# Two-layer recurrent block on one core: early loads by SyncE, v loaded by rows, the scatter in four parts, and the causal mask of the row maxima moved from TensorE to VectorE

## What is computed

```
xn = layernorm(x)                                     # 4096 tokens x 256
q, k, v = xn @ Wq.T, xn @ Wk.T, xn @ Wv.T             # 16 heads of 16
scores = q k^T / 4, masked so that key <= query       # 2 x 16 x 2048 x 2048
out = softmax(scores) @ v, then @ Wo.T
...
logits = xn @ router_w                                # 8 experts, the best one is taken
pos = running count of the tokens of that expert; kept if pos < 512
expert_in[expert, pos] += xn * kept                   # the scatter
hidden = gelu(expert_in @ w1); y = hidden @ w2        # gathered again by (expert, pos)
```

## Time and profile before

| | us |
|---|---|
| median of three executions | 2667.69 (2661.28 to 2670.05) |
| the profiled execution | 2670.18 |
| its span (first to last instruction) | 2668.5 |
| busy in the span: TensorE matmul, VectorE, ScalarE, GpSimd | 2428.0, 1847.2, 1410.9, 938.3 |
| mean granted TensorE clock | 0.952 of full speed |

### The profile page before, as it was taken

How to read it: one execution, slowest core, us unless ns; L and a number is a source line. 1 busy time by engine, 2 the same in 40 slices (tenths; PEclk the granted TensorE clock), 3 DMA queues, 4 the chain that set the end, 5 groups by cost and what they waited for, 6 DMA issues and landing times. The chain is left out here.

```text
span 2668.5 us, 46850 instructions
## 1 busy us (share of the span) xinstructions
PE 2428.0 (91%) x15908; PEld 1558.7 (58%) x15908; DVE 1847.2 (69%) x3682; ACT 1410.9 (53%) x2776; POOL 938.3 (35%) x936
## 2 busy tenths in 40 slices
PE   5778966999999999879967599999999999999999
PEld 4622322333333333268856477777777777777777
DVE  7688865888888888234347567767776777777676
ACT  3525534666666666756533355555555555555554
POOL 2330032110101101024334445555544555544553
PEclk9869978999999999989977799999999999999999
DMA  3850220403404030043266000000000000000000
GB/s 123 228 145 11 43 56 31 62 26 42 60 6 62 17 49 7 15 158 130 75 216 205 11 14 15 9 11 13 13 13 13 13 9 11 13 13 13 13 9 9
DMA packets 180617, 132.47 MB, mean 50 GB/s; under 512 B 91666, under 2 KB 167960, under 8 KB 180497
## 3 DMA queue, kind: packets, MB, share of 16 engines
q1 hardware_dynamic: 149872, 97.96, 14.9%
q0 software_dynamic: 6944, 20.37, 2.6%
q10 hardware_dynamic: 23680, 12.59, 1.8%
HBM read 84.43 MB, written 46.14 MB: 49 GB/s over the span
## 5 line engine op out<-in xcount | busy, mean ns | idle before, releaser
L915 DVE TENSOR_REDUCE a_best<-a_ring 128x1 f32<-128x512 f32 (+3 forms) x1280 | 699.3, 604 | 181.3 <-PE a_ring L716 95.9
L827 ACT ACTIVATE a_probs<-a_pss 128x1024 f32<-128x1024 f32 (+3 forms) x640 | 556.1, 896 | 419.6 <-PE a_pss L766 410.0
L1638 POOL TENSOR_TENSOR w_probs<-w_probs,w_inv 128x512 f32<-128x512 f32 x256 | 301.4, 1177 | 394.3 <-DVE w_inv L1897 385.0
L1803 ACT ACTIVATE w_probs<-w_pss,w_top 128x256 f32<-128x256 f32 x512 | 239.5, 477 | 378.2 <-DVE w_top L1891 363.8
L659 POOL TENSOR_SCALAR_AFFINE_SELECT a_probs<-a_probs 128x256 f32<-128x256 f32 x256 | 102.9, 408 | 785.6 <-ACT a_probs L827 783.8
L1661 PE MATMUL w_psw<-wqkv,w_xr 128*128 128x512 f32 x1152 | 300.5, 397 | 11.6 <-POOL w_xr L1595 11.6
L1701 PE MATMUL w_pss<-w_kd,w_qt 128*128 128x256 f32 x1536 | 277.7, 309 | 0.0
L1891 DVE TENSOR_REDUCE w_top<-w_pss 128x2 f32<-128x512 f32 x256 | 176.9, 691 | 140.6 <-PE w_pss L1701 139.6
L713 PE MATMUL a_ring<-g_kb,g_qa 96*128 96x512 bf16 (+3 forms) x640 | 229.6, 372 | 26.5 <-DVE a_best L915 13.0
L713 PE MATMUL a_ring<-a_kb,a_qa 96*128 96x512 bf16 (+3 forms) x640 | 218.4, 350 | 15.9 <-DVE a_best L915 12.0
L1661 PEld LDWEIGHTS w_psw<-wqkv,w_xr 128*128 128x128 f32 x1152 | 204.8, 189 | 47.4 <-POOL w_xr L1595 12.1
(11 more groups left out here) (233 smaller groups left out, 4187.6 us busy)
## 6 DMA issues: line engine op xcount, KB each, us to landing
e_w<-in_w SPq DMA_DIRECT2D x16, 1024.0 KB, 7.9
qk_parts<-p_parts SPq DMA_DIRECT2D x32, 384.0 KB, 3.9
a_qa<-qk_parts SPq DMA_DIRECT2D x96, 64.0 KB, 2.5
a_kb<-qk_parts SPq DMA_DIRECT2D x24, 256.0 KB, 9.3
g_qa<-qk_parts SPq DMA_DIRECT2D x72, 64.0 KB, 2.5
g_kb<-qk_parts SPq DMA_DIRECT2D x18, 256.0 KB, 8.7
p_xin<-in_x SPq DMA_DIRECT2D x8, 512.0 KB, 5.4
v_rows<-p_vout SPq DMA_DIRECT2D x8, 512.0 KB, 5.3
```

The costliest lines, as they stand in the source:

```text
L827: act.activation(probs[:, idx % 4, :, lo:CH], pss[idx % 2][:, :, lo:CH], ACT.Exp).then_inc(exp_done, 1)
L915: vec.tensor_reduce(best[:, i // TC, h * TC + i % TC, k:k + 1], bank[:, 0:keys], X, ALU.max).then_inc(ring_taken, 1)
L1638: pool.tensor_tensor(probs[:, p % 4, :, :], probs[:, p % 4, :, :], inv[:, :, p:p + 1].to_broadcast([P, 2, 2 * P]), ALU.mult).then_inc(p_re ...
L1803: ins = act.activation(probs[:, p % 4, e, :], pss[p % 2][:, e, :], ACT.Exp, bias=top[:, e, p:p + 1], accum_out=rows[:, e, p:p + 1])
```

## The change

It has four parts.

1. **Early loads.** (Both queues wait first for the stores of chunks 0 to 3.) The first group's loads are no longer issued by GpSimd behind chunk 5's copy, but by SyncE behind chunk 5's store, so ahead of the stores of chunks 6 and 7. TensorE waits once for all 30 of q and k, no longer chunk by chunk.
2. **v by rows, q by heads.** v is one DMA a group instead of four, with runs of 64 floats (256 bytes), into a new tile `v_rows`; GpSimd copies it to `vg` (`place_v`), once per group. q is still 24 DMAs of 64 KB, now one per head and part, not one per chunk and part. Order: k, q, v.
3. **Scatter in parts.** The 32 indirect DMAs go in four lots of 8, at the first step of the last query chunk of groups 3, 4, 5 and 6 (`SCATTER_AT`).
4. **Mask on VectorE.** The matmul L716 is gone. For a diagonal block VectorE reduces the keys ahead of the last 128 as before, if there are any, and then does `tensor_tensor_reduce` on the last 128: adds the float32 mask, writes the sum back to the bank, and takes the maximum into a fifth column of `best`.

```diff
-                if c == NC // B + 1:
...
-                    group_k(pool, dram, [early.kb], 0, early.k_landed)
-                    group_q(pool, dram, [early.qa], 0, early.q_landed)
-                    group_v(pool, dram, [early.vg], 0, early.v_landed)
...
                 store(c, c % 2)
+                if c == NC // B + 1:
...
+                    load_group(sp, dram, [early.qa], [early.kb], [early.v_rows], 0, early.qk_landed, early.v_landed)
...
+    for r, part in enumerate(PARTS_Q):
+        for h in range(GH):
+            eng.dma_start(qa[u][r * HD:(r + 1) * HD, :, h, :],
+                          dram["qk_parts"][0, part, first + h * HD:first + (h + 1) * HD, u * S:(u + 1) * S]
+                          .rearrange("d (c n) -> d c n", n=CH)).then_inc(qk_signal, 16)
+    eng.dma_start(rows[u][:, :, :], dram["v"][u * S:(u + 1) * S, first:first + GH * HD].rearrange("(j p) d -> p j d", p=P)
+                  ).then_inc(v_signal, 16)
...
+            def place_v(g):
+                u = g % 2
+                pool.wait_ge(v_loaded[u] if g else early.v_landed, 16 * ((g + 1) // 2) if g else 16)
+                pool.tensor_copy(vg[u][:, :, :, 0:HD], v_rows[u][:, :, :].rearrange("p j (h d) -> p j h d", d=HD)
+                                 ).then_inc(v_set, 1)
...
+                if s[0] == "S" and s[2:] == (QC - 1, 0, 0):
+                    g = s[1]
+                    if g + 1 < GROUPS:
+                        place_v(g + 1)
+                    if g in SCATTER_AT:
...
+                        for t in range(SCATTER_AT.index(g), NT, len(SCATTER_AT)):
+                            pool.indirect_dma_start(dram["expert_in"],
...
-                if diagonal:
-                    ins = pe.matmul(bank[:, keys - P:keys], keep["identity16"][:, :], keep["mask_qk"][:, :],
-                                    start=False, stop=True)
...
+                    if k < i // TC:
+                        vec.tensor_reduce(found[:, k:k + 1], bank[:, 0:keys], X, ALU.max).then_inc(ring_taken, 1)
+                    else:
+                        own = slice(keys - P, keys)
+                        if keys > P:
+                            vec.tensor_reduce(found[:, k:k + 1], bank[:, 0:keys - P], X, ALU.max)
+                        vec.tensor_tensor_reduce(out=bank[:, own], in0=bank[:, own], in1=keep["mask_qk"][:, :], scale=1.0,
+                                                 scalar=LOWEST, op0=ALU.add, op1=ALU.max, accum_out=found[:, QC:QC + 1]
+                                                 ).then_inc(ring_taken, 1)
```

More of the change, by code:

```diff
@@ L36 @@
 NEG = -1e30
+LOWEST = -3.0e38
 HD = D // H
@@ L317, in _ @@
                 store(c, c % 2)
+                if c == NC // B + 1:
+                    for u in range(2):
+                        for m in range(4):
+                            sp.wait_ge(parts_stored[u][m], 16 * NC // B // 2)
+                        sp.wait_ge(v_stored[u], 16 * NC // B // 2)
+                    load_group(sp, dram, [early.qa], [early.kb], [early.v_rows], 0, early.qk_landed, early.v_landed)
             for u in range(2):
@@ L464 @@
 ROUTE_COUNT, ROUTE_EXP = 6, 8
+SCATTER_AT = (3, 4, 5, 6)
 def attention_plan():
@@ L543, with load_group @@
 RING = 3
[L546 to L556, removed]
+def load_group(eng, dram, qa, kb, rows, g, qk_signal, v_signal):
     first, u = (g // 2) * GH * HD, g % 2
@@ L561, in group_k @@
                       dram["qk_parts"][1, part, first:first + GH * HD, u * S:(u + 1) * S]
[L562 to L571, removed]
+                      .rearrange("(h d) n -> d h n", d=HD)).then_inc(qk_signal, 16)
+    for r, part in enumerate(PARTS_Q):
[5 more added lines that the diff above has]
+                  ).then_inc(v_signal, 16)
 PARTS_Q, PARTS_K = (0, 0, 1, 1, 0, 2), (0, 1, 0, 1, 2, 0)
@@ L584, in __init__ @@
         self.vg = st.sb("vg0", [P, KT, GH, 32])
+        self.v_rows = st.sb("v_rows0", [P, KT, GH * HD])
         self.logits = st.sb("logits", [P, E, NT])
-        self.k_landed, self.v_landed = st.sem("k_landed"), st.sem("v_landed")
-        self.q_landed = [st.sem(f"q_landed{c}") for c in range(QC)]
+        self.qk_landed, self.v_landed = st.sem("qk_landed"), st.sem("v_landed")
         self.set_up = st.sem("set_up")
@@ L708, in a_step @@
                 keys = min(CH, (i + 1) * P - k * CH)
-                diagonal = k == i // TC
                 u, bank = g % 2, ring[r % RING]
                 wait(pe, ring_taken, r + 1 - RING)
-                ins = pe.matmul(bank[:, 0:keys], qa[u][0:QR, i // TC, h, (i % TC) * P:(i % TC + 1) * P],
-                                kb[u][0:QR, h, k * CH:k * CH + keys], start=True, stop=not diagonal)
-                if diagonal:
-                    ins = pe.matmul(bank[:, keys - P:keys], keep["identity16"][:, :], keep["mask_qk"][:, :],
-                                    start=False, stop=True)
-                ins.then_inc(ring_full, 1)
-            pe.wait_ge(early.k_landed, 16 * len(PARTS_K))
-            m = idx = pv = copied = chunk = 0
-            group, ones_seen = 0, -1
-            pe.wait_ge(early.q_landed[0], 16 * len(PARTS_Q))
+                pe.matmul(bank[:, 0:keys], qa[u][0:QR, i // TC, h, (i % TC) * P:(i % TC + 1) * P],
+                          kb[u][0:QR, h, k * CH:k * CH + keys], start=True, stop=True).then_inc(ring_full, 1)
+            pe.wait_ge(early.qk_landed, 16 * n_loads)
+            m = idx = pv = copied = group = 0
+            ones_seen = -1
             for s, r in plan:
@@ L726, in _ @@
                     _, g, h, i, k = s
-                    if g == 0 and i // TC != chunk:
-                        chunk = i // TC
-                        pe.wait_ge(early.q_landed[chunk], 16 * len(PARTS_Q))
                     if g != group:
```

51 lines of the change are left out of this document (19 added, 32 removed).

## The result

The changed kernel takes 2642.78 us (median of 5, 2641.44 to 2648.74), the kernel before beside it 2669.09 (5, 2661.28 to 2670.05): ratio 0.9911, 95% interval 0.9893 to 0.9929. The terms behind that number did not come out alike, though: one was right, two missed in opposite directions and nearly cancelled.

The account below looks back on a forecast made before the run. Neither VectorE nor TensorE was taken to rule an undisturbed group alone, each waiting for the other; the scatter left a 40.3 us hole. Scatter -40.3, loads -2 and mask +28 gave -14 us, hence 2653 us, range 2628 to 2700.

Parts of the forecast that it names:

- Scatter, -40.3 us: In the group with routing: GpSimd's scatter in lots fits its idle time, so PV's whole wait behind it goes, -40.3 us.
- Project and early loads, -2 us: End of project: chunks 4 and 5 run unhindered, but the last stores land behind the loads; -8 to +3, taken as -2 us.
- Rival 4: SyncE's queue: stores of chunks 6 and 7 land late behind the loads, project ends 8 us later; 2661 us, chance 0.06.
- Mask, +28 us: Attention's maxima: VectorE's added instructions cost 0.15 us a diagonal block, partly hidden, less TensorE's saved matmuls; +28 us together.
- r = 0.10: VectorE's accumulator read in each diagonal block, taken to cost 0.10 us, between bounds of 0.065 and 0.199.
- The other sign: Forecast is wrong if VectorE's pass of 128 columns takes more than 1.05 ns a column.
- e: Added VectorE time per diagonal block for the mask: 0.15 us forecast, bounds 0.11 and 0.25.
- TensorE's saving, half of 3.8 us a group: Undisturbed groups: dropping the mask matmuls frees 3.8 us of TensorE's queue a group, of which half was counted.
- Rival 1: VectorE's idle time swallows the mask in groups 1 to 6 at 0.11 us a diagonal block; 2624 us, chance 0.17.
- Rival 2: Accumulator read costs 0.15 us, a diagonal block 0.20 us, mask 44 us; gain and cost cancel at 2670 us, chance 0.14.
- rival 3: VectorE becomes the bound: read 0.20 us, diagonal block 0.25 us, mask +87 us; slower at 2712 us, chance 0.18.
- Rival 5: Scatter lots aren't covered because GpSimd reaches them late; 2653 us plus up to 20, chance 0.03.

## Why the prediction was right, and where it was not

- **Scatter, -40.3 us: right.** -41.8 at the experts' start with nothing else changed, -41.5 in the group itself. The hole goes whole, with the low clock behind it. In the changed kernel the lot of group 3 stands where it was said to: the v copy at 626.73 for 1.04 us, eight scatters from 627.93, 1.29 us apart.
- **Project and early loads, -2 us: wrong, it is +7.2.** The step that failed is the price of the stores behind the loads. I gave the stores behind the loads "2.74 and 1.1 us or up to 4.7 each" and had the last go out at 129 to 135; chunk 6's took 15.45 + 1.10 and the last went out at 143.94. The right price stood in my own: chunk 5's stores, issued beside the loads, take 13.94 us. I counted those 12 us as saved there and did not move them to the chunk that now comes behind the loads. The rest was as worked out: loads from 106.34 (107.4 said, with 4.7 for a chunk's stores where the rows give 2.74 + 1.10) to 122.28 (121 to 125 said). Rival 4 had the mechanism, with 8 us where 9 came. The barrier, "not above 145", was at about 149.3.
- **Mask, +28 us: right in sign, wrong in size; 9.6 to 11.5 by the traces, 11 to 15 by the medians.** The step that failed is the accumulator read: r = 0.10, about 0 found. The prediction's own sign, "wrong if the accumulator read isn't near 0.1 us", came true for the mechanism: its row says 0.14, but that is a duration, and the sum needs the distance of starts. The other sign didn't: the pass of 128 columns runs at a reduction's pace. The parts, mask on VectorE against mask on TensorE: +1.2 for 5.0 ahead of group 0, 2.6 for 7 in group 0, 2.8 for 4 in group 1, 0.2 for 2 in an undisturbed group, and 3.1 in the one group where the clock dips, of which the sum had nothing. VectorE's busy time in such a group, 97.5, is below the 100 that I gave. With e = 0.05, 64 blocks put 3.2 us on VectorE, and 2.1 of them show: more than the 0.4 I took. Two errors, one too large and one too small, meet there.
- **TensorE's saving, half of 3.8 us a group: right**, 1.9.
- **The sum.** -40.3 - 2 + 28 = -14 was forecast. The measured terms are -41.8, +10 to +12 for the loads (+7.2 of it in project) and +9.6 to +11.5 for the mask: -18 to -22, and -20.0 is what the two traces show at the experts' start. Of the 26.3 us between the medians, some 5 arise behind that point. The forecast was right because the mask's error (-17) and the loads' (+13) nearly offset each other. That is luck: of the three terms only the scatter's came out as worked out. The range, with VectorE's bound in it, was wider than it had to be on the slow side.
- **The rivals.** Rival 1 (idle swallows the mask) had the nearest price of the read (0.065 us) but not the result: 2.1 us a group show. Rivals 2 and 3 needed a read of 0.15 and 0.20 us. Where rival 3's price was paid, with the added reduction, its mechanism showed, at 67.5 us instead of 87. (Rival 2's 10.7 and rival 3's 16 for group 0 are 9.8 and 12.6 by the sum's own rule of 0.7 less 1.4; the forecast doesn't rest on either.) Rival 5 did not occur: `PV` never waits over 0.8 us for GpSimd in the kernel after, and one lot of 32 shows that it was far off.

The rule that I had set against the change, from the Trainium skill, "VectorE: DVE Perf Modes" (the section on the TRN2 errata: 120 cycles beside the columns for a PSUM source), would have made e 0.22 us, an estimate from that page. The trace does not agree: 0.05, and an added reduction of 128 columns costs 0.20 us in all, of which 0.13 are its columns at the earlier trace rows's 1.047 ns.

## What to carry to other kernels

A transfer that is moved takes its cost with it: if a burst of loads slows the stores beside it by 12 us now, it will slow those that it is put in front of by as much, and near a barrier nothing hides that. Price such a move with the row in which the two already lie side by side, and start such transfers as early as their inputs allow (here the traces show the gain in project; the median of the earliest start by SyncE doesn't).

A long chain of issues belongs in the longest pause of its own engine. Where it fits there, as 40.9 us did in 40.2, dividing it gained nothing: read the pause itself from that engine's timeline, at the very step where the chain would go. And when some of the edits in a change are worth less than nothing, only kernels with one edit each say so; here the scatter alone was 20 us better than the change, and without a mask in the maximum 29.5 better.

## What the runs showed of the hardware

- VectorE's accumulator read behind an add-and-maximum lasts 0.141 us in the record and costs 0 to 0.04 us between starts. The pass itself takes 0.20 to 0.21 us to the next start for 128 columns, with two operands, one of them in PSUM, and a plain reduction 0.19 to 0.20.
- A group's q, k and v loads (31 DMAs) hold the 16 DMA engines at a share above 1 for some 30 us, at 121 to 127 GB/s where they are alone, while 100 to 110 us of the kernel after moves 224 GB/s at a share of 0.71, and 120 to 130 of the kernel before 291 at 0.84. Four stores issued by SyncE in that time take 15.45 us instead of 2.74, and 13.94 where GpSimd issues the loads.
- TensorE's granted clock fell to 0.50 for 3.3 us twice in group 5 of the kernel after, each time behind a wait for VectorE of 1.59 or 1.90 us, and that group took 3 us longer. Group 4 has the same two waits and kept 1.00.
